# Second pass of a fused attention and gated-linear-attention block: output product of the gated tile one pipeline step later, expert chosen in four operations, late VectorE work in another order

## The reference

```
x = x + layernorm(attn(layernorm(x)))      # 16-head linear attention: one context over all 4096 rows of a batch
x = x + layernorm(ffn(layernorm(x)))
# ffn: two gated linear attentions over chunks of 64 rows, with a running state per head
#   dense path:  q1, k1, v, gk1
#   expert path: q2, k2 times the router's weight; each row belongs to one of 4 experts, each with its own state
o = o_dense + o_sparse                      # sparse: only the row's own expert gives an output
o = o * rsqrt(mean(o*o, per head) + EPS) * norm_w * silu(g)
return o @ Wo
```

## Time and profile before

| | us |
|---|---|
| median of 3 runs | 2894.51 (2893.9 to 2912.56) |
| profiled execution | 2894.36 |
| its span, first to last instruction | 2892.5 |

### The profile page before, as it was taken

How to read it: one execution, slowest core, us unless ns; L and a number is a source line. 1 busy time by engine, 2 the same in 40 slices (tenths; PEclk the granted TensorE clock), 3 DMA queues, 4 the chain that set the end, 5 groups by cost and what they waited for, 6 DMA issues and landing times.

```text
span 2892.5 us, 55901 instructions
## 1 busy us (share of the span) xinstructions
PE 2608.7 (90%) x20208; PEld 1613.3 (56%) x20208; DVE 1987.7 (69%) x4006; ACT 1695.4 (59%) x3345; POOL 923.6 (32%) x750
## 2 busy tenths in 40 slices
PE   6999799989999999999779997998999999999987
PEld 3444466555655666655534444655566665655654
DVE  4442487788777777877644425778877787777786
ACT  4332566666666666666434325666666666666664
POOL 2884222223322233222212241222333223322222
PEclk9999899999999999999889998999999999999999
DMA  5120100000000000000022101000000000000000
GB/s 186 59 90 33 37 23 22 22 22 22 27 25 25 22 22 22 22 22 22 19 88 62 62 32 35 23 22 22 22 22 28 26 22 22 22 22 22 22 22 12
DMA packets 48376, 97.49 MB, mean 34 GB/s; under 512 B 5376, under 2 KB 5376, under 8 KB 47680
## 3 DMA queue, kind: packets, MB, share of 16 engines
q1 hardware_dynamic: 37008, 68.44, 7.3%
q10 hardware_dynamic: 9792, 17.83, 1.7%
q0 software_dynamic: 1520, 10.50, 0.9%
HBM read 63.19 MB, written 33.55 MB: 33 GB/s over the span
## 4 chain that ended last, share of the span: by engine, by line
PE 66%; DVE 23%; issue 7%; ACT 4%; DMA 0%; DVEq 0%; ACTq 0%; SPq 0%
PE psum L303 12%; PE psum L304 11%; PE psum L305 11%; PE psum L581 6%; DVE region L1147 5%; PE psum L437 5%; PE psum L454 4%; PE psum L427 4%; DVE region L1203 4%; PE psum L473 3%; DVE region L1212 2%; DVE region L1144 2%; DVE og L1091 2%; DVE og L1272 2%; DVE region L1223 1%
## 5 line engine op out<-in xcount | busy, mean ns | idle before, releaser
L1007 POOL TENSOR_TENSOR region<-region,kfac 128x512 f32<-128x512 f32 x64 | 66.8, 1043 | 769.1 <-DVE kfac L1231 769.1
L303 PE MATMUL psum<-wb,region 128*128 128x512 f16 x768 | 292.4, 381 | 4.1 <-DVE region L1203 4.1
L304 PE MATMUL psum<-wb,region 128*128 128x512 f16 x768 | 292.5, 381 | 0.0
L305 PE MATMUL psum<-wb,region 128*128 128x512 f16 x768 | 292.3, 381 | 0.0
L995 POOL TENSOR_TENSOR region<-region 128x1024 f32<-128x1024 f32 x64 | 150.2, 2347 | 430.6 <-DVE region L1116 430.6
L990 POOL TENSOR_TENSOR region<-region 128x1024 f32<-128x1024 f32 x64 | 146.5, 2290 | 288.8 <-DVE region L1354 230.7
L1002 POOL TENSOR_SCALAR region<-region,m 128x512 f32<-128x512 f32 x256 | 172.9, 695 | 180.7 <-DVE hm L1184 104.4
L1354 DVE SCALAR_TENSOR_TENSOR region<-psum,region 128x512 f16<-128x512 f32 x64 | 44.3, 692 | 262.0 <-ACT region L830 262.0
L498 PE MATMUL psum<-ident,og 128*128 128x128 f16 x512 | 42.2, 229 | 171.4 <-DVE og L1091 171.4
L1147 DVE SCALAR_TENSOR_TENSOR region<-psum,m,region 128x256 f32<-128x256 f32 x384 | 185.8, 484 | 13.7
L716 ACT ACTIVATE region<-region 128x1024 f16<-128x1024 f32 x64 | 67.7, 1058 | 197.9 <-DVE region L1203 197.9
(11 more groups left out here) (235 smaller groups left out, 7841.8 us busy)
## 6 DMA issues: line engine op xcount, KB each, us to landing
region<-x_in SPq DMA_DIRECT2D x128, 256.0 KB, 2.7
q_cols<-region ACTq DMA_DIRECT2D x64, 256.0 KB, 2.3
region<-q_cols SPq DMA_DIRECT2D x64, 256.0 KB, 2.9
out_rows<-region SPq DMA_DIRECT2D x60, 256.0 KB, 2.0
region<-wb_in POOLq DMA_DIRECT2D x1, 3072.0 KB, 11.8
region<-wqkv_in SPq DMA_DIRECT2D x4, 512.0 KB, 5.6
region<-wqkv_in POOLq DMA_DIRECT2D x2, 1024.0 KB, 5.7
region<-wproj_in POOLq DMA_DIRECT2D x2, 1024.0 KB, 7.5
```

The source lines that it names most:

```text
L303: mm(out, lhs(0), rhs(0), start=start, stop=False)
L304: mm(out, lhs(0), rhs(1), start=False, stop=False)
L305: return mm(out, lhs(1), rhs(0), start=False, stop=stop)
```

## The change

- `og_transpose`, `back_og`, `out_mm`, `back_norm3` and `back_out` now work in step n on tile n-2 (`t`, under a new flag `tail`) and no longer on n-1. The pass gets a further step at its end, and the loop starts one step later. `og_transpose` also waits for the join of tile n-1, since bank 7 is shared. `den`, `project_k2`, `project_k` and `cumulate` wait for a `sel_ok` that counts to four.
- The expert's output is chosen in four operations of 512 elements over banks 0 to 3, after all eight products (one semaphore, ix_pe); the products of banks 2 and 3 still come first.
- `osq` and ScalarE's scratch (`junk`) get buffers of their own. x1 with its mean added goes to a new buffer `xr` (`front_residual`), and `xmean` is doubled.
- ScalarE makes the label before it copies v; `back_rms` comes after the exponentials.
- VectorE: key factors and silu come before the head norm; norm, gating and split of the gated output go to the end of the step, around `back_out` and `front_decay`.
- SyncE stores tile pairs one later behind the loads.

Left out below: buffers and names, the changed counts in `den` and `cumulate`, `ahead_centre`, `back_square`, ScalarE's call of `front_residual`, and the step calls of ScalarE and VectorE, which are those of TensorE.

```diff
@@ -281,12 +282,18 @@
                 j0 = b * (TILES // 2)
                 for p in range(2):
                     load(j0, p)
-                with sp.Fori(b * (TILES // 2) + 1, b * (TILES // 2) + TILES // 2) as j:
+                for p in range(2):
+                    wait_alone(sp, S("x1_ok"), j0 * 2 + 2 + p)
+                    wait_alone(sp, S("qz_ok"), j0 * 2 + 2 + p)
+                    load(j0 + 1, p)
+                with sp.Fori(b * (TILES // 2) + 2, b * (TILES // 2) + TILES // 2) as j:
                     for p in range(2):
                         wait_alone(sp, S("x1_ok"), j * 2 + p)
                         wait_alone(sp, S("qz_ok"), j * 2 + p)
                         load(j, p)
-                        store(j - 1, p)
+                        store(j - 2, p)
+                for p in range(2):
+                    store(j0 + TILES // 2 - 2, p)
             for p in range(2):
                 wait_alone(sp, S(f"out{p}"), BATCH * (TILES // 2 * 16) + 1)
 
...
@@ -321,10 +328,11 @@
                     last = mm3(bank[0], lambda x: qz16[:, x, g, :], lambda x: mix[:, x, g, :], False, g == KT - 1)
                 last.then_inc(S("y_pe"), 1)
 
-            def xn_transpose(n, again=True):
+            def xn_transpose(n, again):
                 pe.wait_ge(S("xn_ok"), cur(n))
                 if again:
-                    pe.wait_ge(S("out_ok"), n)
+                    pe.wait_ge(S("osum_ok"), n)
+                    pe.wait_ge(S("out_ok"), n - 1)
                 for g in range(KT):
                     for part in range(2):
                         at = (part * KT + g) * P
...
@@ -377,13 +385,13 @@
             def project_k2(n, back):
                 pe.wait_ge(S("carry_ok"), prev(n))
                 if back:
-                    pe.wait_ge(S("sel_ok"), (n - 1) * 8 + 4)
+                    pe.wait_ge(S("sel_ok"), (n - 1) * 4 + 4)
                 second(bank[3], 3, 4).then_inc(S("k2_pe"), 1)
 
             def project_k(n, back):
                 pe.wait_ge(S("ldiff_ok"), cur(n))
                 if back:
-                    pe.wait_ge(S("sel_ok"), (n - 1) * 8 + 4)
+                    pe.wait_ge(S("sel_ok"), (n - 1) * 4 + 4)
                 for g in range(KT):
                     mm3(bank[2], lambda x: xnT[:, x, g, :], lambda x: wb[:, x, g, C:2 * C], g == 0, g == KT - 1)
 
...
@@ -464,16 +472,17 @@
                 pe.wait_ge(S("carry_ok"), cur(n))
                 if front:
                     pe.wait_ge(S("ldiff_ok"), cur(n + 1))
-                for half, done in ((0, "ia_pe"), (1, "ib_pe")):
-                    if half and front:
+                for half in (1, 0):
+                    if half == 0 and front:
                         pe.wait_ge(S("v_ok"), cur(n + 1))
                     for r in range(2):
                         for odd in range(2):
                             h = slice(odd * D2, odd * D2 + D2)
-                            last = mm(psum[:, 2 - 2 * half + odd, r * 256:r * 256 + 256], q2T[h, 2 * half + r, :],
+                            last = mm(psum[:, 2 * half + odd, r * 256:r * 256 + 256], q2T[h, 2 * half + r, :],
                                       statex[h, 2 * half + r, :], start=True, stop=True)
-                    last.then_inc(S(done), 1)
-                pe.wait_ge(S("out_ok"), prev(n))
+                last.then_inc(S("ix_pe"), 1)
+                if not front:
+                    pe.wait_ge(S("out_ok"), n)
                 if front:
                     pe.wait_ge(S("same_ok"), cur(n + 1))
                 for pr in range(PAIRS):
...
@@ -490,8 +499,10 @@
                                   start=False, stop=True, skip_group_check=True)
                 last.then_inc(S("o_pe"), 1)
 
-            def og_transpose(n):
+            def og_transpose(n, back):
                 pe.wait_ge(S("og_ok"), cur(n))
+                if back:
+                    pe.wait_ge(S("osum_ok"), cur(n + 1))
                 for g in range(KT):
                     for part in range(2):
                         at = (part * KT + g) * P
...
@@ -523,13 +533,13 @@
                     den(n + 1, mp, back=back)
                 if front:
                     project_q1(n)
-                if back:
-                    og_transpose(m)
+                if tail:
+                    og_transpose(t, back)
                 if front:
                     project_q2(n)
                     cumulate(n, back)
-                if back:
-                    out_mm(m)
+                if tail:
+                    out_mm(t)
                 if front:
                     half_sums(n)
                 if ahead:
...
@@ -622,12 +632,15 @@
                 pe.wait_ge(S("mix_ok"), b * 2 + 2)
                 y_mm(n0)
                 xn_transpose(n0, again=False)
-                step(n0, 0, back=False)
-                with pe.Fori(b * TILES + 1, b * TILES + TILES - 1, 2) as n:
-                    step(n, 1)
-                    step(n + 1, 0)
+                step(n0, 0, back=False, tail=False)
+                step(n0 + 1, 1, tail=False)
+                with pe.Fori(b * TILES + 2, b * TILES + TILES - 2, 2) as n:
+                    step(n, 0)
+                    step(n + 1, 1)
+                step(n0 + TILES - 2, 0)
                 step(n0 + TILES - 1, 1, ahead=False)
                 step(n0 + TILES, 0, front=False, ahead=False)
+                step(n0 + TILES + 1, 1, front=False, back=False, ahead=False)
 
 
         @block.scalar
...
@@ -674,7 +687,11 @@
                 act.wait_ge(S("t_pe"), cur(n))
                 act.wait_ge(S("q1_pe"), prev(n))
                 ac(xnT.rearrange("p x a b -> p (x a b)"), bank16[7], ACT.Copy).then_inc(S("xnT_ok"), 1)
-                ac(x1[:, p, :], x1[:, p, :], ACT.Identity, bias=xmean[:, :]).then_inc(S("x1m_ok"), 1)
+
+            def front_residual(n, p, again):
+                if again:
+                    act.wait_ge(S("out_ok"), n)
+                ac(xr[:, p, :], x1[:, p, :], ACT.Identity, bias=xmean[:, p, :]).then_inc(S("x1m_ok"), 1)
 
             def ahead_z(n):
                 act.wait_ge(S("den_pe"), cur(n))
...
@@ -773,30 +790,31 @@
                 act.wait_ge(S("wo_pe"), cur(n))
                 rstd_of(n, 2, bank[7], eps_scaled)
 
-            def step(n, p, front=True, back=True, ahead=True):
-                m = n - 1
+            def step(n, p, front=True, back=True, tail=True, ahead=True):
+                m, t = n - 1, n - 2
                 if front:
                     front_low(n)
+                    front_label(n)
                     front_v(n, p)
-                    front_label(n)
                     front_gates(n, 0)
                     front_router(n)
                     front_gates(n, 1)
                     front_sig_high(n)
                 if back:
                     back_square(m)
-                    back_rms(m)
                 if front:
                     front_ke(n)
                     front_sig(n)
                 if ahead:
                     ahead_z(n + 1)
-                if back:
-                    back_og(m)
+                if tail:
+                    back_og(t)
                 if front:
                     front_exps(n)
                 if back:
-                    back_norm3(m)
+                    back_rms(m)
+                if tail:
+                    back_norm3(t)
                 if front:
                     front_exs(n, p)
                 if ahead:
...
@@ -1092,7 +1115,7 @@
 
             def ahead_residual(n, p, again=True):
                 if again:
-                    dve.wait_ge(S("out_ok"), n)
+                    dve.wait_ge(S("x1m_ok"), n)
                 dve.wait_ge(S("rstd0"), n + 1)
                 dve.wait_ge(S("xc_ok"), cur(n))
                 ve.scalar_tensor_tensor(x1[:, p, :], bank[0], rstd[:, 0, :], xb[:, p, :], ALU.mult, ALU.subtract).then_inc(S("x1_ok"), 1)
...
@@ -1135,21 +1158,17 @@
             def back_select(n, p):
                 dve.wait_ge(S("osq_ok"), prev(n))
                 dve.wait_ge(S("on_ok"), prev(n))
-                for half in range(2):
-                    dve.wait_ge(S(("ia_pe", "ib_pe")[half]), cur(n))
-                    to = osum[:, half * 256:half * 256 + 256].rearrange("p (h d) -> p h d", h=H2 // 2)
-                    of = psum[:, 2 - 2 * half:4 - 2 * half, :].rearrange("p b (r e d) -> p (b r) e d", r=2, e=NEXP)
-                    for e in range(NEXP):
-                        if e == 0:
-                            step_ = ve.tensor_scalar(to, of[:, :, e, :], m4[:, p, e:e + 1], None, ALU.mult)
-                        else:
-                            dve.wait_ge(S("sel_ok"), n * 8 + half * 4 + e)
-                            step_ = ve.scalar_tensor_tensor(to, of[:, :, e, :], m4[:, p, e:e + 1], to, ALU.mult, ALU.add)
-                        step_.then_inc(S("sel_ok"), 1)
+                dve.wait_ge(S("ix_pe"), cur(n))
+                to = osum.rearrange("p (h d) -> p h d", h=H2)
```

(72 more changed lines are left out.)

18 lines of the change are left out of this document (9 added, 9 removed).

## The result

The changed kernel takes 2744.37 us (median of 4 runs, 2741.56 to 2747.57), the kernel before, in the same comparison, 2897.74. The ratio is 0.946, 95% interval 0.943 to 0.950. The profiled execution took 2741.56 us with a span of 2739.7; the span of before was 2892.5.

What follows compares the result with a forecast made beforehand. TensorE was taken to set the pace, with a large wait before the gated output's transposes. From 2894.4 us, 131 for the steps and pass ends and 20 for the clock were subtracted: 2743, range 2725 to 2800 with 0.8.

Steps and rivals of the forecast that it cites:

- The gap of 2.72 us: TensorE's wait for VectorE's split before the gated output's transposes: goes with the output one step later, 2.72 us a step.
- The choice: Four operations on 512 elements at 0.75 us: TensorE's keys' second product waits for all, costing 0.53 us a step.
- The label: Label first in ScalarE's order: expert products start 0.2 us earlier (bounds 0 and 0.3).
- Step: Sum for a usual step: 34.31 - 2.72 + 0.53 = 32.12 us, a gain of 2.19.
- Slack of VectorE before the residual: 0.8 us before the residual (L1098) hides all of VectorE's late norm, gating, out operation, decay and split.
- Ends: Ends of a pass: step 31 gains 2.9, step 1 2.3, the last two tiles' finish loses 5.4 us.
- Clock: TensorE's clock drops, all behind gaps of 2.56 us or more, taken as gone: 12 x 1.69 = 20 us.
- The first rival: The drops of TensorE's clock stay: 2763 us, chance 0.12.
- The late residual: Rival: VectorE becomes late at the residual, losing 74 us: 2817 us (2800 to 2865), chance 0.12.
- the costly choice: Rival: the choice reads four banks with a stride and costs far more, 2993 us at 1.76 us an operation; chance 0.03.
- nothing is won: Rival: the wait moves, transposes waiting for the join or ScalarE's copy holding the product: 2894 us, chance 0.04.

Runs made afterwards that it cites:

- a_oldorder: Changed kernel with VectorE's norm, norming, gating and split and ScalarE's rms back at their old places, output product still one step later: 2871.1 us.
- a_halves: Changed kernel with the choice again in eight operations, in two halves, project_k2 and project_k waiting for the first four: 2714.1 us.
- a_decaylate: Changed kernel with the small decay product behind the split of the gated output: 2741.4 us.
- b_fill2: Kernel before with eleven idle wide products filling TensorE's gap before the transposes of the gated output: 2870.3 us, ratio 0.987.
- b_label2: Kernel before with only the label ahead of v on ScalarE: 2913.3 us, ratio 1.001.
- b_four2: Kernel before with only the choice of the expert in four operations: 2871.6 us, ratio 0.987.
- b_fill_three: Kernel before with three idle wide products in the gap before the transposes of the gated output: 2872.6 us, ratio 0.988.

## Why the prediction was right

2743 was predicted, 2744.4 measured. That the two are so near is partly luck: steps 1 to 30 gained, without the clock, 2.5 us a batch less than predicted (65.5 in place of 68.0), and the rest of the kernel gained about 6 us more than predicted. Term by term:

- The gap of 2.72 us. Gone, as said. But I gave all of it to the later output product and costed VectorE's new order at nothing, hidden. a_oldorder shows that the move needs the order: with the product moved and the old order, TensorE waits 1.8 us for y instead; that the order needs the move is read from the waits in the code. The sum is right, for both parts are in the change; read as a price of the move alone it is wrong by 1.9 us of 2.72.
- The choice. Start 2.14 us behind the expert products (2.23 predicted), 0.75 us an operation as taken from the pointer-scalar row, end at 2338.89. Counted from the last gate product, the keys' product starts 6.07 us behind it after and 5.49 before: 0.58 us later, predicted 0.53. That the four operations are a loss for TensorE was the step's point, and undoing them shows it: 0.49 us a step in a_halves, 0.66 where the residual is in time.
- The label. Predicted 0.2, measured 0.11 by undoing it. TensorE starts the expert products 0.25 us after the carry's end (2333.40 to 2333.65), where I had taken 0.12.
- Step: 34.31 - 2.72 + 0.53 = 32.12 predicted, 32.16 measured.
- Slack of VectorE before the residual: predicted 0.8, measured 0.27. The order was hidden as said, but two operations ran longer than their rows, 0.88 for 0.69 and 1.42 for 0.69, beside GpSimd's work. I had priced moved work by durations from a place where nothing overlapped it. The 0.88 stands beside GpSimd's key product (L1034) in a_decaylate too, and was not tried without it. It cost nothing, since the slack held; 0.3 us more and it would have, as a_halves shows.
- Ends. Step 1 takes 31.05 us, a gain of 3.3 where I had 2.2 + 2.3. The last join to the last out operation takes 16.5 us (2719.98 to 2736.52), predicted 18.7, before 13.3: I took a slow product for tile 30, as in the kernel before (about 4.3 us from 2883.48), and it ran at the full clock (2722.54 to 2725.15, 2.6 us), as this profile shows:

```profile
2722.54 0.39 PE L310 MATMUL psum<-wo,ogT 128*128 128x512 f16 x1 [1.12 <-ACT ogT L787]
...
2724.93 0.38 PE L312 MATMUL psum<-wo,ogT 128*128 128x512 f16 x1
```

- Clock. Predicted 20 us for 12 slow steps. In the profiled executions it is 8.3 + 9.9 in the steps and about 2.6 in step 31 of the first batch (the expert products behind it start 25.9 us after the step's log-sigmoid, 23.3 in the second batch), all gone. The first rival (the drops stay) falls with that and with b_fill2. What was not foreseen is that the loss isn't fixed: over the comparisons the kernel before had medians of 2897.7 to 2907.5, and with the label alone moved the profile has 26 slow steps in place of 11. The reason that the prediction gave for "gone" (all drops followed gaps of 2.56 us or more) was too narrow: a_oldorder has drops behind 1.81 us, which no idle time of the changed kernel's usual step reaches.
- The late residual and the costly choice did not come; "nothing is won" is what a_oldorder came near to, but through the y product and not through the join, a place that I hadn't named.

Without the clock the predicted gain was 131 us, and the measured one 152.8 - 20.8 = 132.

## What to carry to other kernels

When a stall is taken off the bounding engine, it can come back at the next thing that the engine which caused it owes, as it did here with the old order; name that next thing before giving the gain to one of the edits. Fewer and longer operations can cost the bounding engine more than they save the other one, when it waits for their first part only; keep the part that is waited for first short and with a semaphore of its own. Price moved work by what will run beside it at its new place.

## What the runs showed of the hardware that I had not expected

- An idle time of TensorE of 2.56 us in every step lets the granted clock fall to its lower level in some steps (11 of 60 in the profile of before, 26 of 60 in that of b_label2). One of 1.9 us at the same place did so in none of 60 (b_four2, b_fill_three), one of 1.8 us before the y product in 2 of 60 (a_oldorder). A slow step is 1.4 to 1.7 us longer than a usual one. Filling the gap with useless products gained 33 us of 2903.
- A VectorE subtraction with both inputs in SBUF took 1.42 us beside GpSimd's tensor product and 0.69 without it; GpSimd's took 2.36 and 1.91. The cast from SBUF in the old order took 1.16 us in place of 0.43; GpSimd's key product was running when it started, but this was not tried by itself.
